# A twelve-stage decoder on one core: the position attention on row groups, and the history branch with channels on partitions

## The chip, the cores and the metric

One core of one Trainium2 chip runs the whole program. Its engines work side by side and are tied by semaphores: TensorE (PE, with its weight loads as PEld), VectorE (DVE), ScalarE (ACT), GpSimd (POOL) and SyncE (SP), which issues the DMAs. The metric is the device time of one execution in microseconds; the median of three runs is given. Of a profiled execution there is a trace, with the span from its first to its last instruction.

## The reference

Four decoder layers with three sublayers each (self attention, cross attention, feed forward), each followed by a layer norm of x plus its result. x is 8 batches of 100 tokens with 256 channels, the context 8 batches of 361 rows. Two sublayers matter here.

The feed forward of layer 1 begins with an attention of 16 heads of 16 channels that has relative positions:

```
x = _layernorm(src, ln1_g, ln1_b)
q, k, v = x @ wq, x @ wk, x @ wv         (16 heads)
p = (pe @ wp).reshape(2 * Ss - 1, H, HD)
ac = jnp.einsum('bihd,bjhd->bhij', q, k)
bd_full = jnp.einsum('bihd,phd->bhip', q, p)
rel = jnp.arange(Ss)[:, None] - jnp.arange(Ss)[None, :] + (Ss - 1)
bd = bd_full[:, :, jnp.arange(Ss)[:, None], rel]
att = jax.nn.softmax((ac + bd) * scale, axis=-1)
src = src + (att @ v) @ wo
x2 = _layernorm(src, ln2_g, ln2_b)       (then the experts)
```

There are 199 positions for 100 tokens, so bd_full is 100 x 199 for each head and batch, and each row of it is read shifted by one against the row above.

The cross attention of layer 2 takes from the context (the history) a summary for each batch, from which a small net makes 3x3 kernels for the attention scores:

```
eh = _gelu(_ln(historical_data @ hist_W + hist_b, hist_ln_g, hist_ln_b))   (361 x 512)
aw = _gelu(eh @ ctx_W1 + ctx_b1) @ ctx_W2 + ctx_b2                          (361)
aw = jax.nn.softmax(aw, axis=1)
cc = jnp.sum(eh * aw, axis=1)                                               (512)
```

## The kernel before

The stages (the functions in `STAGES`) run one after another. Each stage is one or more blocks; inside a block every engine has its own list of instructions, in the order written out by hand, and at the end of a block the engines meet. `stage_sems` gives a block its semaphores; with `looped=True` a block is repeated by a register loop (`Fori`), with a barrier of all engines between the turns. PSUM has 8 banks of 512 floats. Matmuls are in float32, and each stands in the trace as two records. The weights of the next stage are loaded by SP at the start of each stage.

**Position stage (`l1_ffn`, L2846).** In a first block the norm runs batch by batch (L2880 on), `pT` (positions times weights) is made, each batch is turned to channels on partitions (`x1T`), and then all queries are projected into `q1` (L2900, L2912). A loop of two turns with four batches each follows. In it GpSimd spreads the queries (L2937): for each head a copy of all 128 rows in which the other heads' rows are zero. TensorE multiplies each of the 16 heads with `pT` over all 128 rows (L2955), two heads in a PSUM bank; VectorE (L2927) and ScalarE (L2929) copy the banks in turn; SP stores each half batch to DRAM (L2972), in rows of 199 floats at a pitch of 200, and at the end of the turn waits until the stores have landed. The buffer `bd` holds two batches. After the loop `attention` (L184) runs, the generic one for all eight batches: it projects again, spreads the queries once more on GpSimd (L375), makes scores over 128 rows (L484), and adds the positions that SP loads back for each batch (L343), 100 floats at a time through the skewed view `skewed`; a separate instruction takes the maxima (L675, L678).

**The row-group attention (`self_heads`, L1172)** is used by the stages `l0_attn` and `l2_xattn`. It keeps the queries of even and odd heads apart in `q_pad`, so that a product needs only 32 rows; the four groups of 32 rows work on four banks (L1315). The masked scores and their maxima come from one instruction for each head (L1499), the exponentials from ScalarE (L1424), and turned probabilities are copied by VectorE and ScalarE in turn (L1508, L1433). What is small shares one side bank (projection of values L1279, inverses L1289, output L1294, turned x L1299), in the order of `side_order`.

**History branch (`l2_xattn`, L3201).** A first block loads the bias, gain and shift rows (`hist_rows`, on all partitions) and stores zeros for the taps. Then come two turns of a loop with four batches each. Tokens are on partitions, in three tiles of 121, 121 and 119. GpSimd copies the context (L3261), TensorE projects it (L3277), VectorE adds the bias, takes the statistics and normalises (L3341 to L3352), ScalarE applies gelu (L3320), TensorE turns the tiles to channels on partitions (L3287) and ScalarE copies them (L3324). The first layer (L3293), its gelu (L3327) and the logits (L3297, one row of 361) follow. The softmax runs on one partition (L3355 to L3362), its result is turned to a column (L3301, L3366), and TensorE sums the tokens of the four batches (L3306), 48 records with 512 columns over both turns. The result is turned to `ccT` (L3311, L3334). The block behind the loop makes the kernels from it (L3397 on).

## Time and profile before

| | us |
|---|---|
| median of 3 runs | 2757.68 |
| lowest, highest | 2756.59, 2758.4 |
| profiled execution | 2755.74 |
| its span | 2753.6 |
| PE busy | 2334.3 (85%) |
| PEld busy | 1864.6 (68%) |
| DVE busy | 1540.1 (56%) |
| ACT busy | 1138.2 (41%) |
| POOL busy | 516.5 (19%) |

The mean TensorE clock that was granted is 0.915 of full speed. Busy time is the union of an engine's instructions; TensorE's ends are modelled, so that a busy TensorE is not one at its peak. The shares are means over twelve stages with different limits, and a stage has to be read by itself.

### The profile page before, as it was taken

The numbers are of one execution on the slowest core, as the hardware profiler recorded it, in microseconds if no ns is written. First come the engines' busy times: TensorE is split into PE (matmuls) and PEld (weight loads), VectorE is DVE, ScalarE is ACT, GpSimd is POOL, SyncE is SP. The second block draws the span as 40 slices with busy tenths as digits, with TensorE's granted clock in tenths as the row PEclk, the third lists the DMA queues.
The fourth block names the chain that finished last, engine by engine and source line by source line (L and its number), as shares of the span: only waits on it lengthen the run. The fifth ranks groups of instructions, "written<-read, shape, count | busy, mean of one in ns | idle before, by whom it ended". The sixth has DMA issues, their size and how long they took to land. (4 is left out here: it accounts for less than half of the span.)

```text
span 2753.6 us, 43435 instructions
## 1 busy us (share of the span) xinstructions
PE 2334.3 (85%) x15392; PEld 1864.6 (68%) x15392; DVE 1540.1 (56%) x3310; ACT 1138.2 (41%) x3111; POOL 516.5 (19%) x715
## 2 busy tenths in 40 slices
PE   5799556669999966979787787979997999799997
PEld 3566322247777755879775336869995566599997
DVE  4566649984444432755556453545654556555555
ACT  5566345534334422623211233434332466455553
POOL 0200119961000023300133111000003222100000
PEclk9899779999999978979888888979997999799999
DMA  2000122210000034234200004422210000233332
GB/s 105 9 2 2 37 83 72 71 51 5 1 1 1 1 96 110 48 106 150 97 1 16 0 1 111 120 73 94 98 41 32 5 8 4 64 109 109 109 104 64
DMA packets 57520, 152.12 MB, mean 55 GB/s; under 512 B 16983, under 2 KB 31931, under 8 KB 55304
## 3 DMA queue, kind: packets, MB, share of 16 engines
q1 hardware_dynamic: 57356, 149.99, 17.4%
q8 instruction: 96, 1.57, 0.2%
q14 instruction: 68, 0.56, 0.1%
HBM read 138.48 MB, written 11.50 MB: 54 GB/s over the span
## 5 line engine op out<-in xcount | busy, mean ns | idle before, releaser
L2302 PE MATMUL ps<-l1a_zc,tables_sb 128*128 128x400 f32 x256 | 107.6, 553 | 96.3 <-POOL l1a_zc L2231 60.3
L2302 PEld LDWEIGHTS ps<-l1a_zc,tables_sb 128*128 128x128 f32 x256 | 46.9, 200 | 157.0 <-POOL l1a_zc L2231 88.5
L1799 ACT ACTIVATE l1x_probs<-ps,l1x_nmax 100x361 f32<-100x361 f32 x128 | 70.8, 558 | 189.1 <-DVE l1x_nmax L1881 189.1
L2242 POOL TENSOR_TENSOR l1a_dbx<-l1a_dx,l1a_rows 128x400 f32<-128x400 f32 x128 | 129.9, 1045 | 7.0 <-DMA l1a_rows<-l1a_rows_spilled 4.9
L2650 DVE TENSOR_TENSOR l3f_act_out<-l3f_act_out,l3f_gates 128x800 f32<-128x800 f32 x80 | 79.4, 992 | 81.9 <-ACT l3f_act_out L2606 81.9
L2654 DVE TENSOR_TENSOR l3f_hg_low<-l3f_act_out,l3f_hg_high 128x800 fp32r<-128x800 f32 x80 | 79.4, 993 | 62.9 <-ACT l3f_hg_high L2612 62.9
L2606 ACT ACTIVATE l3f_act_out<-ps,l3f_biases 128x800 f32<-128x800 f32 x80 | 74.4, 930 | 91.8 <-PE ps L2495 91.8
L2494 PE MATMUL ps<-l3f_x_high,l3f_w_high 128*128 128x400 f32 x320 | 111.4, 348 | 0.0
L2493 PE MATMUL ps<-l3f_x_high,l3f_w_low 128*128 128x400 f32 x320 | 110.7, 346 | 0.5 <-DVE l3f_w_low L2584 0.5
L2495 PE MATMUL ps<-l3f_x_low,l3f_w_high 128*128 128x400 f32 x320 | 110.8, 346 | 0.0
L2494 PE MATMUL ps<-l3f_hg_high,l3f_w_high 128*128 128x400 f32 x320 | 110.2, 344 | 0.0
L2255 ACT ACTIVATE ps<-l1a_delta,weights 128x400 f32<-128x400 f32 x128 | 76.5, 598 | 81.1 <-DVE ps L2285 53.1
L2493 PE MATMUL ps<-l3f_hg_high,l3f_w_low 128*128 128x400 f32 x320 | 110.1, 344 | 0.0
L2495 PE MATMUL ps<-l3f_hg_low,l3f_w_high 128*128 128x400 f32 x320 | 110.0, 344 | 0.0
L1024 ACT ACTIVATE l3x_probs<-l3x_s_sb,l3x_nmax 100x361 f32<-100x361 f32 x128 | 75.2, 589 | 70.3 <-DVE l3x_nmax L1113 66.3
L2612 ACT ACTIVATE l3f_hg_high<-l3f_act_out 128x800 fp32r<-128x800 f32 x80 | 70.0, 875 | 72.3 <-PE ps L2495 70.0
L1022 ACT ACTIVATE l0x_probs<-ps,l0x_nmax 100x361 f32<-100x361 f32 x128 | 70.8, 558 | 64.9 <-DVE l0x_nmax L1120 56.7
L2494 PE MATMUL ps<-l2f_x_high,l2f_w_high 128*128 128x400 f32 x272 | 95.0, 349 | 0.0
L2495 PE MATMUL ps<-l2f_x_low,l2f_w_high 128*128 128x400 f32 x272 | 94.4, 347 | 0.0
L2493 PE MATMUL ps<-l2f_x_high,l2f_w_low 128*128 128x400 f32 x272 | 94.3, 347 | 0.0
L2285 DVE TENSOR_TENSOR_SCAN ps<-ps,l1a_dbx 128x400 f32<-128x400 f32 x86 | 84.6, 994 | 16.6 <-POOL l1a_dbx L2242 9.8
L1113 DVE CUSTOM_DVE_ANT_0 l3x_s_sb<-ps,l3x_mask_b 100x361 f32<-100x361 f32 x128 | 63.2, 532 | 46.6 <-PE ps L929 46.3
(666 smaller groups left out, 6641.5 us busy)
## 6 DMA issues: line engine op xcount, KB each, us to landing
l3f_landing<-l_ffn_units SPq DMA_DIRECT2D x40, 513.0 KB, 3.4
l3f_gates<-l3f_gates SPq DMA_DIRECT2D x40, 400.0 KB, 3.5
l2x_a_taps<-l2x_taps_spread SPq DMA_DIRECT2D x8, 1912.5 KB
l2f_landing<-l_ffn_units SPq DMA_DIRECT2D x17, 771.0 KB, 4.3
l1a_rows<-l1a_rows_spilled SPq DMA_DIRECT2D x32, 400.0 KB, 3.2
l1f_gates<-l1f_gates SPq DMA_DIRECT2D x16, 800.0 KB, 4.2
l1f_positions<-l1f_bd SPq DMA_DIRECT2D x16, 621.9 KB
l1f_landing<-l_ffn_units SPq DMA_DIRECT2D x16, 512.0 KB, 3.5
```

The source lines that it names most:

```text
L1022: last = act.activation(probs[:, n % 2, r, 0:KEYS], score_bank(r), ACT.Exp, bias=nmax[:, n % 2, r:r + 1], accum_out=sums)
L1024: last = act.activation(probs[:, n % 2, r, 0:KEYS], s_sb[:, h % 3, r % 2, :], ACT.Exp, scale=-1.0, bias=nmax[:, n % 2, r:r + 1], accum_out ...
L2242: pool.tensor_tensor(dbx[:, n % BUFS, :], dx[:, j, m, :], rows[:, g % RING, 0, :], ALU.mult).then_inc(s.dbx_ready, 1)
L2255: act.activation(da(n), delta_h[:, m, j, :], ACT.Exp, scale=a_log[:, m, i:i + 1]).then_inc(s.da_ready, 1)
L2285: dve.tensor_tensor_scan(z(n), da(n), dbx[:, n % BUFS, :], 0.0, ALU.mult, ALU.add).then_inc(s.scan_done, 1)
L2302: pe.matmul(y_bank(m), st.ident, zc[:, n % DONE, :], start=(i == 0), stop=(i == NS - 1)).then_inc(s.sum_done, 1)
L2493: pe.matmul(out, r(w_lo), r(x_hi), start=start, stop=False)
L2494: pe.matmul(out, r(w_hi), r(x_hi), start=False, stop=False)
L2495: return pe.matmul(out, r(w_hi), r(x_lo), start=False, stop=stop)
L2606: act.activation(halves(act_out, t), st.ps[:, bank:bank + 2, 0:HALF], ACT.Gelu, bias=col(sl, 2 + t if geglu else t)).then_inc(s.gelu_done, 1)
L2650: dve.tensor_tensor(hg[:, t, :], act_out[:, t, :], gates[sl][:, 0, :], ALU.mult).then_inc(s.hg_gated, 1)
L2654: dve.tensor_tensor(hg_low[:, t, :].bitcast(F32R), hg[:, t, :], hg_high[:, t, :], ALU.subtract).then_inc(s.hg_ready, 1)
```

## The change

**Position stage.** The separate query projection, the loop over two turns and the call of `attention` are gone; `l1_ffn` calls `self_heads` with three new arguments: `xT` (the normed x, turned), `inner` (gain and shift of the second norm, and where its turned result goes) and `between` (the positions). The stage's norm block stays. In `self_heads` the products with the positions are made in 32 parts, four for each batch, each with four products over 32 rows (two row groups, two banks). The 12 parts of the first three batches stand ahead of the value projection and use four pairs of banks; those of batch j + 3 are woven into batch j, all in banks 0 and 1, which the scores use too, and each of them waits until both halves of the part before it are copied. VectorE copies the first bank of a part and ScalarE the second into `staged`, which holds three units of two parts. SP stores a unit in rows of 8 x 199 floats without a gap, and loads a batch of the skewed view into `bd` (two batches) when both its units have landed and the maxima of the batch two before are done. The position takes the place of the mask in the instruction of L1499. GpSimd adds the resid to x; VectorE's norm gets its gain and shift.

**History branch.** The first block and the loop become one block that runs all eight batches. Channels are on partitions: four products of 361 columns for each batch, straight from `ctxT`. The mean is taken out of the weights and of the bias beforehand (`w_centred`, `b_centred`), so that only the variance is left to find: VectorE squares, GpSimd adds the four channel tiles, TensorE sums over partitions into three columns, GpSimd raises to the power -0.5 and widens, TensorE spreads the result over all partitions. VectorE multiplies, and ScalarE's gelu takes gain and shift as its scale and bias. Logits are made on all 128 partitions. The exponentials of all batches and the weighted sums (VectorE, 32 with an accumulator) stand behind the loop. `hist_rows` is no longer loaded; three groups of four columns in the weights take its place.

The core of the diff (indentation halved):

```diff
-def self_heads(nc, st, name, w, bias=None, mask=None, conv=None):
+def self_heads(nc, st, name, w, bias=None, mask=None, conv=None, xT=None, inner=None, between=None):
...
+      bd_bank = lambda part: 2 * (part % 4) if part < 4 * AHEAD else 0
+      bd_tile = lambda part, i: st.ps[0:S, bd_bank(part) + i, 0:2 * REL]
+      staged_tile = lambda part, i: staged[:, part // 2 % STAGED, 4 * (part % 2) + 2 * i:4 * (part % 2) + 2 * i + 2, :].rearrange("q h r -> q (h r)")
...
+      def load(sp, j):
+        for unit in (2 * j, 2 * j + 1):
+          sp.wait_ge(bd_stored[unit % STAGED], 16 * (unit // STAGED + 1))
+        if j >= 2:
+          sp.wait_ge(s.masked_ready, G * (j - 1))
+        sp.dma_start(bd[:, j % 2], between.skewed(j)).then_inc(bd_loaded[j % 2], 16)
+      if between:
+        @block.sync
+        def _(sp):
+          for j in range(B):
+            if j >= AHEAD:
+              load(sp, j - 1)
+            for unit in (2 * j, 2 * j + 1):
+              sp.wait_ge(s.bd_first_copied, 2 * unit + 2)
+              sp.wait_ge(s.bd_second_copied, 2 * unit + 2)
+              sp.dma_start(between.rows(j)[:, (unit % 2) * (H // 2):(unit % 2 + 1) * (H // 2), :], staged[:, unit % STAGED]).then_inc(bd_stored[unit % STAGED], 16)
+            if j < 2:
+              load(sp, j)
+          for j in range(LOADED, B):
+            load(sp, j)
...
+        def positions(part):
+          j, q = divmod(part, 4)
+          m = q // 2
+          if part % (4 * HALF) == 0:
+            pe.wait_ge(s.q_even_copied, KT * (j // HALF + 1))
+            pe.wait_ge(s.q_odd_copied, KT * (j // HALF + 1))
+          if part >= 4 * AHEAD:
+            pe.wait_ge(s.masked_ready, G * (j - AHEAD) + 2)
+            pe.wait_ge(s.bd_first_copied, part)
+            pe.wait_ge(s.bd_second_copied, part)
+          elif part >= 4:
+            pe.wait_ge(s.bd_first_copied, part - 3)
+            pe.wait_ge(s.bd_second_copied, part - 3)
+          for par in range(2):
+            for i in range(2):
+              r = 2 * (q % 2) + i
+              group = slice(SLOT * r, SLOT * (r + 1))
+              last = pe.matmul(st.ps[0:S, bd_bank(part) + i, par * REL:(par + 1) * REL], q_pad[group, par, m, j, :], between.pT[group, m, :],
+                      start=True, stop=True, tile_position=(SLOT * r, 0))
+          last.then_inc(s.bd_ready, 1)
...
+          for part in range(4 * AHEAD):
+            positions(part)
+          pe.wait_ge(s.bd_first_copied, 4 * AHEAD)
+          pe.wait_ge(s.bd_second_copied, 4 * AHEAD)
         project("v", 0, 0)
...
             values(j - 1)
+          more = between and j + AHEAD < B
+          if more:
+            positions(4 * (j + AHEAD))
+          if 1 <= j <= B:
             on_the_side("inv", j - 1)
+          if more:
+            positions(4 * (j + AHEAD) + 1)
           if j < B:
             if conv:
               convolve(G * j + 2)
             turn(G * j)
+          if more:
+            positions(4 * (j + AHEAD) + 2)
           if j + 1 < B:
             on_the_side("v", j + 1)
           if j < KT:
             on_the_side("k", 1, j)
+          if more:
+            positions(4 * (j + AHEAD) + 3)
           if not conv and j + 1 < B:
             scores(j + 1)
...
+        def copy_positions(part):
+          act.wait_ge(s.bd_ready, part + 1)
+          wait_staged(act, part)
+          act.activation(staged_tile(part, 1), bd_tile(part, 1), ACT.Copy).then_inc(s.bd_second_copied, 1)
...
+          if between and r == 0:
+            dve.wait_ge(bd_loaded[j % 2], 16 * (j // 2 + 1))
           for n in range(G):
-            last = dve.tensor_tensor_reduce(s_sb[:, g % 3, n, :], score_bank(r)[:, n, :], conv.mask if conv else mask, 1.0, -3 * MASKED,
+            if between:
+              add = bd[:, j % 2, head(r, n), :]
+            else:
+              add = conv.mask if conv else mask
+            last = dve.tensor_tensor_reduce(s_sb[:, g % 3, n, :], score_bank(r)[:, n, :], add, 1.0, -3 * MASKED,
                             ALU.add, ALU.min, nmax[:, g % 3, n:n + 1])
...
-
-      w = weights(st, "f5")
-      attention(nc, st, "l1f", H, 16, False, w, xT=x1T, inner=InnerNorm(st.w["f5g2"][0:S, :], st.w["f5s2"][0:S, :], x2T), bd=skewed, per_turn=B)
-
+        return bass.AP(tensor=scratch.tensor, offset=b * S * PITCH + S - 1, ap=[[PITCH - 1, S], [REL, H], [1, S]])
+      self_heads(nc, st, "l1f", weights(st, "f5"), xT=x2T, inner=InnerNorm(st.w["f5g2"][0:S, :], st.w["f5s2"][0:S, :], x2T),
+           between=Between(pT=pT, rows=position_rows, skewed=skewed))
...
+          def widen(n):
+            pool.wait_ge(s.var_copied, n + 1)
+            pool.tensor_tensor(hrstd[:, n % 2, :], hvar[:, n % 2, :], st.minus_half[0:KROWS, 0:1].to_broadcast([KROWS, NT]), ALU.pow).then_inc(s.rstd_done, 1)
+            pool.wait_ge(s.rstd_done, n + 1)
+            if n >= 2:
+              pool.wait_ge(s.rstd_spread, n - 1)
+            pool.tensor_copy(rstd_wide[:, n % 2], hrstd[:, n % 2, :].unsqueeze(2).to_broadcast([KROWS, NT, P])).then_inc(s.rstd_widened, 1)
...
+          for n in range(B + 1):
+            if n < B:
+              pool.wait_ge(s.squared, 2 * n + 1)
+              pool.tensor_tensor(sq[:, n % 2, 0, :], sq[:, n % 2, 0, :], sq[:, n % 2, 1, :], ALU.add).then_inc(s.half_summed, 1)
+            if n >= 1:
+              widen(n - 1)
+            if n < B:
+              pool.wait_ge(s.squared, 2 * n + 2)
+              pool.tensor_tensor(sq[:, n % 2, 2, :], sq[:, n % 2, 2, :], sq[:, n % 2, 3, :], ALU.add).then_inc(s.half_summed, 1)
+              pool.wait_ge(s.half_summed, 2 * n + 2)
+              if n >= 2:
+                pool.wait_ge(s.var_ready, n - 1)
+              pool.tensor_tensor(sq_sum[:, n % 2, :], sq[:, n % 2, 0, :], sq[:, n % 2, 2, :], ALU.add).then_inc(s.sq_summed, 1)
...
+          def project(n):
             for c in range(CT):
+              if n >= 1:
+                pe.wait_ge(s.eh_copied, CT * (n - 1) + c + 1)
+              for k in range(KT):
+                last = pe.matmul(st.ps[:, c, 0:KEYS], w_hist[:, k, c * P:(c + 1) * P], st.ctxT[:, n, k, :], start=(k == 0), stop=(k == KT - 1))
+              last.then_inc(s.eh_ready, 1)
...
+          for n in range(B + 3):
+            if n < B:
+              project(n)
+            if 1 <= n <= B:
+              variances(n - 1)
+            if n >= 3:
+              if n == 3:
+                pe.wait_ge(s.w2_widened, 1)
+              attention_logits(n - 3)
+            if 2 <= n <= B + 1:
+              first_layer(n - 2)
+            if 1 <= n <= B:
+              spread(n - 1)
         @block.scalar
...
+          def copy_out(n, c):
+            act.wait_ge(s.eh_ready, CT * n + c + 1)
...
+            act.activation(buf(n)[:, c, :], st.ps[:, c, 0:KEYS], ACT.Identity, bias=b_centred[:, c:c + 1]).then_inc(s.eh_copied, 1)
+          def gelu(n, c):
+            if c == 0:
+              act.wait_ge(s.normed, n + 1)
+            act.activation(buf(n)[:, c, :], buf(n)[:, c, :], ACT.Gelu, scale=hg[:, c:c + 1], bias=hs[:, c:c + 1]).then_inc(s.eh_done, 1)
...
+          for n in range(B + 3):
+            old = n - 2
+            if n < B:
+              copy_out(n, 0)
+            if 0 <= old < B:
+              gelu(old, 0)
+              gelu(old, 1)
+            if n < B:
+              copy_out(n, 1)
+              copy_out(n, 2)
+            if 0 <= old < B:
+              gelu(old, 2)
+              gelu(old, 3)
+            if n < B:
+              copy_out(n, 3)
+            if 0 <= old < B:
+              gelu_first(old)
+          for n in range(B):
+            exponentials(n)
...
+          def normalise(n):
+            dve.wait_ge(s.rstd_spread, n + 1)
+            dve.wait_ge(s.squared, 2 * n + 2)
+            dve.tensor_tensor(buf(n), buf(n), st.ps[:, RSTD_BANK, 0:KEYS].unsqueeze(1).to_broadcast([P, CT, KEYS]), ALU.mult).then_inc(s.normed, 1)
+          def summary(n):
+            dve.wait_ge(s.aw_exp, n + 1)
+            for c in range(CT):
+              dve.scalar_tensor_tensor(buf(n)[:, c, :], buf(n)[:, c, :], 1.0, aw[:, n, :], ALU.mult, ALU.mult, accum_out=ccT[:, c, n:n + 1]).then_inc(s.cc_summed, 1)
...
+          for n in range(B + 3):
+            if 2 <= n <= B + 1:
+              normalise(n - 2)
+            if n < B:
+              square(n, 0)
+            if 1 <= n <= B:
+              copy_variances(n - 1)
+            if n < B:
+              square(n, 1)
+            if 3 <= n <= B + 2:
+              logits(n - 3)
+          for n in range(B):
+            summary(n)
```

## Rows read from the trace of the kernel before

**Rows 1.** Timeline of the position stage: start, us, engine, line [idle before <-releaser].

```profile
986.91 0.34 ACT L2909 ACTIVATE l1f_x1T<-ps 128x200 f32<-128x200 f32 x1 [0.90 <-PE ps L146]
...
1016.60 1.05 DVE L2927 COPY l1f_bd<-ps 100x398 f32<-100x398 f32 x2 [2.94 <-DMA l1f_positions<-l1f_bd]
...
1017.23 5.64 PE L2955 MATMUL ps<-l1f_pT,l1f_q_between 128*100 128x199 f32 x32 [0.81 <-DVE l1f_bd L2927]
...
1193.36 0.34 ACT L567 ACTIVATE l1f_x2T<-ps 128x200 f32<-128x200 f32 x1 [6.74 <-PE ps L459]
```

**Rows 2.** Busy us (x instructions) of PE, PEld, DVE, ACT, POOL; PEclk, DMA share, GB/s.

```profile
50.00:86.00 36.00, 27.82 (x404) 20.83 (x396) 27.41 (x176) 29.95 (x150) 5.54 (x15) 0.95 0.01 3
...
1012.00:1015.00 3.00, 3.00 (x20) 2.95 (x19) 0.89 (x2) 1.00 (x2) 1.08 (x1) 1.00 0.68 192
...
1069.00:1088.00 19.00, 6.31 (x31) 5.79 (x32) 0.00 (x0) 1.23 (x4) 5.85 (x4) 0.64 0.41 97
...
1085.00:1087.00 2.00, 2.00 (x7) 1.45 (x7) 0.00 (x0) 0.25 (x1) 2.00 (x2) 0.50 0.77 144
...
1088.00:1177.00 89.00, 81.17 (x789) 76.97 (x789) 67.62 (x144) 57.61 (x290) 29.66 (x32) 0.99 0.25 52
...
1495.00:1572.00 77.00, 62.16 (x188) 29.43 (x188) 41.05 (x88) 21.93 (x44) 13.14 (x16) 0.85 0.00 0
```

**Rows 3.** Waits of DVE and ACT in the two stages: us in total, times, longest.

```profile
DVE l1f_s_sb L675 <- DMA l1f_bd_cur<-l1f_positions: 20.1, 1, 20.1
...
ACT l2x_cc L3332 <- PE ps L3306: 31.2, 2, 15.6
```

**Rows 4.** Timeline of the history branch.

```profile
1489.36 0.44 POOL L3240 MEMSET l2x_zeros<- 100x408 f32 x1 [1.09 <-POOLq L88]
...
1537.33 1.41 DVE L3352 SCALAR_TENSOR_TENSOR l2x_eh<-l2x_eh,l2x_hrstd,l2x_hist_rows 119x512 f32<-119x512 f32 x2 [0.59 <-POOL l2x_hrstd L3267]
...
1544.49 5.13 PE L3293 MATMUL ps<-l2x_ehT,weights 128*128 128x361 f32 x16
...
1553.10 3.53 PE L3301 MATMUL ps<-tables_sb,l2x_aw 1*121 1x1 f32 x24 [2.06 <-DVE l2x_aw L3362]
...
1649.76 1.28 ACT L3411 ACT_TABLE_LOAD   x1 [0.80 <-PEq L88]
```

**Rows 5.** Timeline of the L0 attention.

```profile
14.83 7.56 PE L1274 MATMUL ps<-XT,weights 128*128 128x400 f32 x16 [14.83 <-PEq L3670]
...
24.80 0.26 DVE L1499 CUSTOM_DVE_ANT_0 l0a_s_sb<-ps,tables_sb 100x100 f32<-100x100 f32 x1 [1.08 <-PE ps L1315]
...
59.51 0.66 PE L1289 MATMUL ps<-tables_sb,l0a_rinv_wide 100*128 100x100 f32 x4 [0.72 <-POOL l0a_rinv_wide L1264]
...
61.63 0.96 PE L1315 MATMUL ps<-l0a_kT,l0a_q_pad 32*100 32x100 f32 x32
...
67.78 0.66 PE L1289 MATMUL ps<-tables_sb,l0a_rinv_wide 100*128 100x100 f32 x4 [0.71 <-POOL l0a_rinv_wide L1264]
...
111.19 0.34 ACT L1415 ACTIVATE XT<-ps 128x200 f32<-128x200 f32 x1 [5.38 <-PE ps L1299]
```

**Rows 6.** Groups by line: busy us, mean ns | idle before <-releaser; window as in rows 1, 5.

```profile
L2927 DVE COPY l1f_bd<-ps 100x398 f32<-100x398 f32 x32 | 18.0, 572 | 64.0 <-PE ps L2955 49.9 <-DMA l1f_positions<-l1f_bd 14.1
...
L2929 ACT ACTIVATE l1f_bd<-ps 100x398 f32<-100x398 f32 x32 | 15.6, 501 | 56.5 <-PE ps L2955 44.9 <-DMA l1f_positions<-l1f_bd 11.6
...
L1424 ACT ACTIVATE l0a_probs<-l0a_s_sb,l0a_nmax 100x100 f32<-100x100 f32 x128 | 46.5, 368 | 3.2 <-DVE l0a_nmax L1499 3.2
```

**Rows 7.** Groups by line: L1 stage, history branch.

```profile
L1784 ACT ACTIVATE l1x_kT<-ps,weights 128x361 f32<-128x361 f32 x64 | 35.9, 561 | 5.8 <-PE ps L1687 5.8
...
L1901 DVE TENSOR_TENSOR l1x_x_low<-ctxT,l1x_x_high 128x722 fp32r<-128x722 f32 x8 | 7.3, 910 | 13.4 <-ACT l1x_x_high L1819 13.4
...
L3267 POOL TENSOR_TENSOR l2x_hrstd<-l2x_hvar,minus_half 121x2 f32<-121x2 f32 x12 | 12.8, 1066 | 1.0
...
L2242 POOL TENSOR_TENSOR l1a_dbx<-l1a_dx,l1a_rows 128x400 f32<-128x400 f32 x128 | 129.9, 1045 | 7.0 <-DMA l1a_rows<-l1a_rows_spilled 4.9
```

More of the change, by code:

```diff
@@ L36 @@
 InnerNorm = namedtuple("InnerNorm", "gain shift turned")
+Between = namedtuple("Between", "pT rows skewed")
 Convolution = namedtuple("Convolution", "windows keep mask")
@@ L1193, in self_heads @@
         r_sb, o_norm = sb("r_sb", [P, 2, KT * S]), sb("o_norm", [P, 2, KT * S])
+        if inner:
+            norm.xnew = norm.resid
+        staged = sb("staged", [S, STAGED, H // 2, REL]) if between else None
+        bd = sb("bd", [S, 2, H, S]) if between else None
         kept = sb("kept", [S, 3, G, S + 2]) if conv else None
@@ L1437, in _ @@
                 copy_q(0)
+                if between:
+                    for part in range(4 * AHEAD):
+                        copy_positions(part)
                 for j in range(B + 2):
@@ L1451, in _ @@
                         copy_out("inv", j - 1)
+                    more = between and j + AHEAD < B
+                    if more:
+                        copy_positions(4 * (j + AHEAD))
                     if j == 0:
@@ L1527, in _ @@
                 copy_q(0)
+                if between:
+                    for part in range(4 * AHEAD):
+                        copy_positions(part)
                 copy_values(0)
@@ L1546, in _ @@
                         add_output(j - 2)
+                    more = between and j + AHEAD < B
+                    if more:
+                        copy_positions(4 * (j + AHEAD))
                     if j < B:
                         maxima(G * j + (1 if conv else 2))
+                    if more:
+                        copy_positions(4 * (j + AHEAD) + 1)
+                    if j < B:
                         if conv:
@@ L1551, in _ @@
                     if j >= 2:
-                        normalise_vector(dve, norm, s, j - 2)
+                        if inner:
+                            dve.wait_ge(s.x_summed, j - 1)
+                        normalise_vector(dve, norm, s, j - 2, *((inner.gain, inner.shift) if inner else ()))
                     if j < B:
@@ L3208, in l2_xattn @@
     w_k2 = st.w["a7kw2"].rearrange("p (k n) -> p k n", k=KT)
-    rows = [min(KROWS, KEYS - t * KROWS) for t in range(NT)]
     LINE = (3 * H + 2) * TAP_PITCH
@@ L3363, in _, with square @@
-                    for j in js:
-                        dve.wait_ge(s.p_turned, j + 1)
-                        for t in range(NT):
-                            dve.tensor_copy(pcol[0:rows[t], j, t, j:j + 1], st.ps[0:rows[t], bank(j, 0), t:t + 1]).then_inc(s.p_col, 1)
+                    def square(n, half):
+                        both = slice(2 * half, 2 * half + 2)
+                        dve.wait_ge(s.eh_copied, CT * n + 2 * half + 2)
+                        if n >= 2 and half == 0:
+                            dve.wait_ge(s.sq_summed, n - 1)
+                        dve.tensor_tensor(sq[:, n % 2, both, :], buf(n)[:, both, :], buf(n)[:, both, :], ALU.mult).then_inc(s.squared, 1)
```

377 lines of the change are left out of this document (151 added, 226 removed).

## The prediction

> **What bounds the kernel now.** I read the busy time by stretch first, to find the two stages that the change touches; then the waits inside them; then the timeline; then the durations of single instructions. Stages run one behind the other with a block switch between them, so the time of the program is the sum of its stages, and what a stage loses or gains moves everything behind it. Two stages count.
>
> The position stage runs from 987.25 (the last turned copy of the first norm ends) to 1193.70 (the last turned copy of the second) [rows 1]: 206.4 us. No engine is full in it outside 1088 to 1177, where TensorE is busy 81 of 89 us in the generic attention; from 1069 to 1088 it works 6.3 of 19 us at a mean clock of 0.64 [rows 2], and VectorE's first add waits 20.1 us for the first load of the skewed positions [rows 3]. So the stage is a front of some 100 us (query projection, two turns of the position loop with its stores drained at each end, block switches, first load), and 8 batches behind it.
>
> The history branch is entered at 1489.36 and the block behind it begins at 1649.76 [rows 4]: 160.4 us, in two like turns of 77 us. In one, TensorE is busy 62 us, VectorE 41, ScalarE 22 [rows 2]: the engines take turns, and ScalarE waits 31.2 us in two pieces for the weighted sums of L3306 [rows 3], which run with four result rows each.
>
> **The position stage after the change.** It removes the separate query projection, the masks of GpSimd, both turns of the loop and the generic attention; it adds the L0 stage's row-group attention with position products woven in. That attention is in the trace: from its first projection (14.83) to its last copy (111.53) are 96.7 us, 10.0 of them ahead of the first maxima at 24.80, and one batch in the steady middle takes 67.78 − 59.51 = 8.3 us [rows 5]. I put it at 987.25 + 1.05 for the block switch = 988.3.
>
> Front. The 12 parts of three batches are computed ahead of the first scores. Copies of query halves end at about +9 (24.80 − 14.83 less the value projection). A part is 8 records; the same product at 128 rows runs at 5.64/32 = 0.18 us a record [rows 1], 1.4 us a part in a row; but two row groups alternate, and four of them do the 32 records of the scores in 0.96 us [rows 5]. I take 0.9 for a part; bounds 0.7 and 1.6. The two copies (0.57 on VectorE, 0.50 on ScalarE [rows 6]) are beside each other. So three units (two parts each) are staged by about +14; the fourth copy has to wait for a store. Before, stores moved 192 GB/s and the load 144 GB/s [rows 2], so 637 KB take 3.4 us and 640 KB 4.4 us of transfer, and the first two stores, begun after the copies at 1006, were waited for until 1016.60 [rows 1]: I take 4 to 5 us from issue to landing. SyncE issues in order: store 0 and 1, then load 0, which waits for both (+17.5), and only behind it store 2; its landing (+22 to +25) frees the buffer for unit 5, whose copies end at +24 to +27; then come the value projection and the scores. The first maxima come at about +28 where L0 has +10: 18 us added. Bounds: 14 (the stores, in pieces eight times as long as before, are twice as quick) and 28 (each transfer takes 7 us).
>
> Batches. Five batches carry the products of a batch three ahead. I walk one, from the end of its scores, by the program's order. ScalarE: a turned copy behind TensorE's transposes (ends 1.1), the turned x (1.45), four exponentials of 0.37 [rows 6] (2.95), a turned copy (3.7). TensorE: values 0.9 (4.6), part 0 (5.5), inverse 0.7 [rows 5] (6.2). ScalarE: inverse copy, part copy (7.15). Part 1 until 8.1; ScalarE is in four exponentials until 8.65, its copy until 9.2; part 2 until 10.1. VectorE: copy of part 1 until 8.7, norm with gain and shift 1.4, four maxima of 0.26 [rows 5] 1.0, turned copy 0.6, so that its copy of part 2 ends at 12.2; part 3 until 13.1; copies until 13.7; the next scores 1.0. Sum 14.7 us. The path goes eight times between TensorE and the copiers, since all later parts share bank pair 0. Below it lie VectorE's own work (L0's 27.4 us in 36 [rows 2] are 6.3 a batch; 6.3 + 4 × 0.57 + 0.9 = 9.5 us) and the transfers (2 × 3.4 + 4.4 = 11.2 us); above it a serial part (4 × 0.5 more, 17). Five batches: 5 × (14.7 − 8.3) = 32. Three plain ones get 0.5 each for gain and shift, the last two norms 0.85 each: 3.2. End: 988.3 + 96.7 + 18 + 32 + 3 = 1138.2, against 1193.7: **55.5 us gained**; bounds 31 (front 28, batch 17, and the rest as it is) and 78 (front 14, batch 11).
>
> A rule that speaks against it: the Trainium skill, "TensorEngine Tiling (Array Packing)", Key Properties, says that a change of tiling mode drains the engine. Here the row-group scores start with no idle time ahead of them [rows 5]. Eight more changes in each of five batches, each costing one record of 0.18 us, would be 7 us.
>
> **The history branch after the change.** Removed: the first block's load and its switch (1489.36 to the loop), copies to hist_cur, transposes (c on the other axis now), one-row softmax and its turning, weighted sums on TensorE, the second turn's fill. TensorE per batch: 8 projection, 4 first-layer and 1 logit products of 361 columns, 26 records at 5.13/16 = 0.32 us = 8.3; three narrow variance products, 6 records at 3.53/24 = 0.15 = 0.9 [rows 4]; the spread, 6 records at 0.66/4 = 0.17 [rows 5] = 1.0. Together 10.2. ScalarE: 9 activations with bias at 0.56 [rows 7] = 5.0. VectorE: two squares at 0.91 [rows 7], one product of twice that width 1.8, variances and logits 1.3: 4.9. GpSimd: three adds of 361 columns (1.05 for 400 [rows 7]: 2.8), a power of three columns (1.07 for two [rows 7]: 1.6), widening 0.5: 4.9. All lie below TensorE's 10.2, and by the program's order each result is ready when TensorE asks (variances read squares of the batch before, first layer those of two before). So TensorE is the bound: 8 × 10.2 = 81.6.
>
> Around it: block start and the centring of weights on VectorE 4.0 (not in the trace; two to six); the first products at half clock, 3; the second iteration waits for the first power, 2.5; the drain (normalise, four gelus, first layer, gelu, logit, maximum) leaves bubbles of 4. Then a tail: all sums stand behind the last logits on VectorE, 32 of them. A like instruction of 512 columns takes 1.41/2 = 0.70 [rows 4], so 0.5 to 0.8 with its accumulator read; I take 0.6: 19.2. ScalarE's exponentials keep ahead of it. With 1.5 for the last steps and the switch: 4 + 3 + 2.5 + 81.6 + 4 + 19.2 + 1.5 = 115.8, against 160.4: **44.6 us gained**; bounds 30 and 55.
>
> **Sum.** The profiled execution took 2755.74 us (span 2753.6); 2755.7 − 55.5 − 44.6 = 2655.6. The median of the runs is 1.9 above it: 2657.6, so 2658.
>
> **Rivals.**
> **Quicker positions** (0.14): the copies find gaps, and a batch costs only the larger of VectorE and transfers, 11 (3.7 × 5 = 18.5 less), with a front 4 shorter. For it: before, one batch with products of all 128 rows took 11 us (89/8) [rows 2]. Against: the single bank pair. 55.5 + 18.5 + 4 = 78; time 2635.
> **Slower ring** (0.18): parts run serially and the SyncE order (a load that waits for maxima stands ahead of stores) holds the three-unit ring. 10 more in front, 14 in the batches: 2682. For it: before, the copies already waited for stores [rows 1].
> **Table switches** (0.04): if Identity with bias and Gelu did not share a table set, six loads of 1.28 us [rows 4] in each batch put ScalarE at 12.7 and, with the path, a batch at 13.5: 27 more, 2685. Against: no row shows the pair; the L1 stage has Identity with bias 64 times among exponentials at 0.56 us and 5.8 us of idle time in all [rows 7], so a second set is not needed there. The Trainium skill, "ScalarE: Activation LUTs", counts identity among the cheap functions that every set holds; by that rule the loop needs no load between them, which this trace cannot show.
> **Slower than before** (0.02): the granted clock stays at the lower level (1.2 GHz) in both stages. History: 10.2 more per batch, 82. Positions: some 6 us of the batch's path are TensorE's, 5 × 6 + 12 + 4 = 46. Together 128, net 28 slower: 2786. It decides from about three quarters of both stretches at that level. Against: 0.95 in L0's middle at 28 of 36 us busy, 0.85 in the history turn now [rows 2], which gets fuller.
>
> **How the numbers follow.** Forecast 0.60, with its own range 2640 to 2675; the rest is two in a hundred for terms of both stages falling together outside. The range runs from just below the quicker rival, 2632, to past the slower ones, 2692. This kernel's measurement tells 0.2% (5.5 us) from no change. Faster 0.97, same 0.01, slower 0.02.
>
> **What would show it.** Position stage near 150 us from its first norm copy: first maxima 28 after the first projection, maxima of batches one to four some 14.7 apart, the last three some 9; VectorE and ScalarE part copies waiting for TensorE, and in the front for stores. History: TensorE over 95% busy in the middle at clock 1.00, batches 10.2 apart, then 20 us of VectorE alone. Wrong if sums overlap the loop, if products of two row groups take over 1.4 us a part, if a table load stands between Identity and Gelu, or if the loop's pace is set by GpSimd.

## The result and the profile after

The changed kernel takes 2671.45 us (median of four runs, 2660.57 to 2675.93) against 2758.04 us for the kernel before on the same chip: a ratio of 0.968, 95% interval 0.965 to 0.971. Forecast were 2658, range 2632 to 2692. The profiled execution took 2672.13 us, its span is 2670.3 against 2753.6, so 83.3 us went. By stage:

| | before | after | gained | forecast |
|---|---|---|---|---|
| position stage, from the last turned copy of the first norm to that of the second | 206.4 | 173.3 | 33.2 | 55.5 |
| history branch, block start to next block | 160.4 | 105.4 | 55.0 | 44.6 |
| all stages ahead | 987.2 | 992.8 | −5.5 | 0 |
| between and behind | 1399.5 | 1398.8 | 0.7 | 0 |

The 5.5 us ahead are put down to scatter: the same instructions stand there, the stage's first projection begins anywhere from 987.3 to 995.3 us in the twelve profiles of this study that hold the new stage, and the run with the old stage and the new history branch reaches the end of the first norm at 992.4 too, where the kernel before had 987.2.

The head of the page of the changed kernel, busy time and two rows in 40 slices:

```profile
span 2670.3 us, 42999 instructions
...
PE 2268.9 (85%) x15178; PEld 1804.2 (68%) x15178; DVE 1497.1 (56%) x3444; ACT 1137.8 (43%) x3097; POOL 474.6 (18%) x697
...
PE   6799674659999976869987959899987999799998
...
PEclk8899787899999986669978979989988999799999
```

The sixteenth to eighteenth slices are the position stage: three 6s in the clock, where the page of before has no 6 at all. The same by stretch (columns as in [rows 2]): front; batches 0 and 1, which also carry the projections of batches 4 to 7; batches 2 to 4, the three others with parts (the recorded expectations call them "three to five"); and the rest.

```profile
992.80:1026.60 33.80, 17.78 (x144) 11.99 (x148) 7.72 (x15) 7.34 (x16) 0.95 (x1) 0.70 0.34 103
1026.60:1067.00 40.40, 32.67 (x204) 19.08 (x203) 14.40 (x81) 18.37 (x79) 0.40 (x1) 0.65 0.42 121
1067.00:1117.80 50.80, 41.44 (x399) 29.36 (x394) 27.51 (x141) 26.95 (x119) 5.45 (x12) 0.72 0.36 103
1117.80:1166.00 48.20, 34.18 (x324) 24.77 (x316) 27.09 (x143) 24.06 (x114) 8.76 (x19) 0.64 0.13 40
```

The third number from the end is the granted clock: 0.64 to 0.72, 0.68 over the whole stage, where L0's attention, from which I took the durations, has 0.95 [rows 2], and where the generic attention that was replaced had 0.99 [rows 2]. A clock of 0.68 is a mixture of TensorE's two levels, 2.4 and 1.2 GHz. The timeline of TensorE in one batch shows where it changes (start, us, engine, line, in brackets the idle time ahead and what ended it):

```profile
1104.82 0.89 PE L1423 MATMUL ps<-l1f_probsT,l1f_vals 100*32 100x100 f32 x32 [0.64 <-issue]
1105.65 0.92 PE L1367 MATMUL ps<-l1f_pT,l1f_q_pad 32*100 32x199 f32 x8
1107.38 0.66 PE L1337 MATMUL ps<-tables_sb,l1f_rinv_wide 100*128 100x100 f32 x4 [0.82 <-POOL l1f_rinv_wide L1308]
...
1110.79 1.65 PE L1367 MATMUL ps<-l1f_pT,l1f_q_pad 32*100 32x199 f32 x8
1112.38 2.03 PE L1327 MATMUL ps<-weights,l1f_xT 128*100 128x256 f32 x4
1114.34 1.65 PE L1367 MATMUL ps<-l1f_pT,l1f_q_pad 32*100 32x199 f32 x8
1116.66 1.67 PE L1387 MATMUL ps<-l1f_kT,l1f_q_pad 32*100 32x100 f32 x32 [0.68 <-DVE l1f_staged L1580]
```

L1367 is a part of the positions, L1327 the value projection, L1387 the scores. A part takes 0.92 us early in the batch (I had taken 0.9) and 1.65 us late in it, which is over the 1.4 us that I had named as a sign of being wrong; the scores take 1.67 instead of the 0.96 of [rows 5]. All these stand on the path, and the waits between them are short: none of TensorE's is over 0.92 us in these three batches. The last of the three took 17.3 us from scores to scores (1099.4 to 1116.7), the two ahead of it 15.6 and 17.2.

In the front, VectorE's copies of parts show the transfers (columns as in the timeline above):

```profile
1002.86 2.97 DVE L1580 COPY l1f_staged<-ps 100x398 f32<-100x398 f32 x6 [2.35 <-PE ps L1367]
1010.40 1.05 DVE L1580 COPY l1f_staged<-ps 100x398 f32<-100x398 f32 x2 [4.58 <-DMA l1f_positions<-l1f_staged]
1012.90 1.05 DVE L1580 COPY l1f_staged<-ps 100x398 f32<-100x398 f32 x2 [1.44 <-DMA l1f_positions<-l1f_staged]
1021.57 1.05 DVE L1580 COPY l1f_staged<-ps 100x398 f32<-100x398 f32 x2 [7.62 <-DMA l1f_positions<-l1f_staged]
...
1027.10 0.26 DVE L1615 CUSTOM_DVE_ANT_0 l1f_s_sb<-ps,l1f_bd 100x100 f32<-100x100 f32 x1 [1.93 <-PE ps L1387]
```

The first projection starts at 993.13, so the first maxima come 34.0 us behind it; L0 had 10, the forecast was 28.

The history branch, TensorE's timeline at its start and in the steady middle (L3328 projection, L3336 variances, L3343 logits, L3350 first layer, L3358 spread):

```profile
1465.54 12.88 PE L3328 MATMUL ps<-ctxT,weights 128*128 128x361 f32 x32 [1.59 <-DVE weights L3461]
...
1520.59 5.03 PE L3328 MATMUL ps<-ctxT,weights 128*128 128x361 f32 x16
1525.46 0.69 PE L3336 MATMUL ps<-l2x_ones,l2x_sq_sum 128*121 128x1 f32 x6
1526.02 0.85 PE L3343 MATMUL ps<-l2x_g1T,l2x_w_wide 128*128 128x361 f32 x2
1526.71 2.60 PE L3350 MATMUL ps<-l2x_eh,weights 128*128 128x361 f32 x8
1529.14 0.83 PE L3358 MATMUL ps<-tables_sb,l2x_rstd_wide 121*128 121x121 f32 x6
1529.80 5.03 PE L3328 MATMUL ps<-ctxT,weights 128*128 128x361 f32 x16
```

No gap, and 9.2 us from batch to batch. The first stretch below lies in this steady middle, the second behind the loop: there TensorE stands still, VectorE is full with the sums, and ScalarE has only 4 us of exponentials (columns as in [rows 2]):

```profile
1507.00:1520.00 13.00, 13.00 (x56) 8.84 (x55) 6.78 (x10) 6.09 (x12) 7.09 (x10) 1.00 0.01 2
...
1553.00:1568.30 15.30, 0.00 (x0) 0.00 (x0) 14.90 (x67) 3.98 (x15) 0.00 (x0) 0.51 0.00 0
```

VectorE's sums as a group (columns as in [rows 6]):

```profile
L3453 DVE SCALAR_TENSOR_TENSOR l2x_eh<-l2x_eh,l2x_aw 128x361 f32<-128x361 f32 x32 | 14.6, 529 | 0.0
```

### The profile page after: what moved, and what is told of

Its sections match the earlier page's. It is cut to its first block and busy times, and to the rows that moved or that the text cites. A ratio compares the mean times of both kernels' runs of the same rounds, so it can differ in the third digit from the quotient of the medians.

```text
span 2670.3 us, 42999 instructions
## 1 busy us (share of the span) xinstructions
PE 2268.9 (85%) x15178; PEld 1804.2 (68%) x15178; DVE 1497.1 (56%) x3444; ACT 1137.8 (43%) x3097; POOL 474.6 (18%) x697
## 3 DMA queue, kind: packets, MB, share of 16 engines
q1 hardware_dynamic: 46012, 149.21, 17.3%
```

## The experiments

Theory A: the position stage is 22 us longer than forecast because TensorE runs much of it at the lower clock, with a smaller part from the order of transfers in the front. Rival B: the path of copies through one bank pair and the transfers set the batch, and the clock is low because TensorE waits for them. Each ratio is to the kernel before on the same chip, with its 95% interval; "stage" is the time from the stage's first projection to the end of its last turned copy, 172.9 us in the changed kernel, and "block" the history branch's, 105.4.

| | median us | ratio | stage | block |
|---|---|---|---|---|
| changed kernel | 2671.45 | 0.9678 (0.9648 to 0.9709) | 172.9 | 105.4 |
| history branch alone | 2702.49 | 0.9793 (0.9778 to 0.9808) | | 105.1 |
| position stage alone | 2725.76 | 0.9882 (0.9864 to 0.9900) | | |
| products that nobody reads | 2657.63 | 0.9631 (0.9614 to 0.9647) | 164.5 | |
| their waits alone | 2670.68 | 0.9678 (0.9662 to 0.9695) | 178.1 | |
| store first | 2663.51 | 0.9652 (0.9639 to 0.9665) | 166.4 | |
| keys in front | 2660.58 | 0.9646 (0.9627 to 0.9665) | 167.4 | |
| keys and queries in front, store first, GpSimd's order | 2651.02 | 0.9613 (0.9595 to 0.9630) | 152.7 | 104.8 |
| sums in the drain | 2674.57 | 0.9682 (0.9659 to 0.9704) | | 107.4 |
| sums in the steady state | 2667.36 | 0.9679 (0.9657 to 0.9701) | | 105.7 |
| all together | 2641.96 | 0.9577 (0.9552 to 0.9601) | 146.7 | 107.3 |
| all, mended | 2639.90 | 0.9564 (0.9540 to 0.9589) | 142.7 | 105.3 |
| all, four units | 2641.73 | 0.9578 (0.9562 to 0.9594) | 144.3 | 105.6 |

**Each part of the change alone.** The one kernel keeps `l1_ffn` of before, the other `l2_xattn`.

> The history branch of the changed kernel with the position stage of the kernel before. Both theories of this study concern the position stage, so this run prices the two parts. If the traces' stage lengths are the two gains (history branch 105.4 us against 160.4 us, position stage some 33 us shorter), this kernel is 55 us below the kernel before, at 2703, and some 32 us above the changed kernel. If a part of the gain belongs to the clock that a stage leaves behind for the next, the difference is under 50 us.

> The position stage of the changed kernel with the history branch of the kernel before. If the two gains add, the history branch being worth 56.8 us by its own run, this kernel is at 2671 + 57 = 2728, some 30 us below the kernel before. If one stage leaves the other a better or worse clock, they differ from this sum by more than 4 us.

The history branch alone gives 56.8 us, the position stage alone 33.5; together 90.3, where the whole change gave 86.6 against the kernel before on its own chip. They agree with the stage lengths (55.0 and 33.2) and add within 4 us.

**Products that nobody reads, and the waits without them.** On TensorE, at five places of each batch:

```diff
+                def keep_busy(bank):
+                    if between:
+                        pe.matmul(st.ps[:, bank, 0:256], w.o[:, 0, 0:P], w.v[:, 0, 0:256], start=True, stop=True)
...
                 def values(j):
+                    if j > 0:
+                        pe.wait_ge(s.o_ready, j)
+                        keep_busy(O_BANK)
                     pe.wait_ge(s.even_copied, 2 * j + 2)
...
+                    if between and j + 1 < B:
+                        pe.wait_ge(s.masked_ready, G * (j + 1))
+                        keep_busy(3)
                     if more:
                         positions(4 * (j + AHEAD) + 3)
```

Each product goes to a bank that no other engine reads by then, and for that some waits move ahead of it. The second kernel has these waits with an empty `keep_busy`.

> Products whose results nobody reads, each 128 rows by 256 columns (some 0.55 us at the higher clock), are put in the position stage at the five places of a batch where TensorE waits: ahead of the values, of the inverse, of the second and the fourth part of the positions and of the scores. Theory A (the granted clock made my batch of 14.7 us one of 17.2): the clock of the stage rises from 0.70 to over 0.9, batches with parts take 14.5 to 15.5 us, the stage is 8 to 15 us shorter and the time is about 2661. Rival B (the path of copies and transfers sets the batch, the clock is low because TensorE waits): the five products lie partly on the path, the batch stays at 17 to 19 us and the time is 2671 to 2685.

> The waits of the run with products that nobody reads, moved as there (the values wait for the output first, and the fourth part and the scores for all maxima), without the products. If the products did it by way of the clock (theory A), this kernel is as the changed one: batches of 17.2 us, clock 0.70, scores at 1.67 us, time 2669 to 2673. If the other order of waits did it (rival B), batches three to five are at 14 to 16 us here too and the time is about 2661.

The stretches of batches 2 to 4 of both kernels, with the products and with the waits alone (columns as in [rows 2]):

```profile
1069.00:1113.20 44.20, 39.41 (x407) 26.80 (x406) 27.68 (x143) 27.30 (x119) 5.44 (x12) 0.95 0.38 114
```

```profile
1068.00:1124.00 56.00, 48.20 (x371) 33.55 (x367) 27.84 (x141) 27.28 (x119) 5.47 (x12) 0.57 0.31 90
```

With the products the clock is 0.95, the scores take 0.96 us, and the three batches take 14.0, 14.3 and 15.9 us; VectorE, ScalarE and GpSimd do the same work in both. With the waits alone the clock is 0.57 and the batches take 18.6, 17.2 and 20.3 us, 6 us more together than in the changed kernel, though the time is the same; of the 13.6 us of stage between the two kernels, 8.4 are therefore what the products gain over the changed kernel. The intervals of the two ratios don't meet: 13 us of time between kernels that differ only in work whose result is thrown away. That is theory A, and it shows my 14.7 us for a batch as right at the higher clock. What the products do not do is help batches 0 and 1: they stay at 21.3 and 20.6 us, at clocks of 0.61 and 0.67. There the projections of batches 4 to 7 (L1322) stand between copies, 5.3 us for the queries and 3.0 for each part of the keys, where L0 took 2.95 for the queries, 3.04 and 1.61 for the two parts of the keys.

**Store first.** SyncE issues the stores of units 2 and 4 ahead of the loads:

```diff
                             sp.dma_start(between.rows(j)[:, (unit % 2) * (H // 2):(unit % 2 + 1) * (H // 2), :], staged[:, unit % STAGED]).then_inc(bd_stored[unit % STAGED], 16)
-                        if j < 2:
-                            load(sp, j)
+                            if unit in (2, 4):
+                                load(sp, unit // 2 - 1)
```

> SyncE issues the store of unit 2 ahead of the load of batch 0, and that of unit 4 ahead of the load of batch 1. Theory C (SyncE's order holds the three-unit ring in the front): the store of unit 2 goes out at 7.5 us after the first store's place instead of 9.3, unit 5 is copied some 4 to 5 us earlier, the first maxima come 5 us earlier (29 us behind the first projection instead of 34) and the time is 2666.5. Rival D (the bytes set the front: three stores and one load have to pass whatever their order): the first maxima stay within 1 us of 34 and the time is 2670 to 2672.

VectorE's copies in that kernel, whose first projection starts at 988.27:

```profile
1005.54 1.05 DVE L1580 COPY l1f_staged<-ps 100x398 f32<-100x398 f32 x2 [4.68 <-DMA l1f_positions<-l1f_staged]
1008.25 1.05 DVE L1580 COPY l1f_staged<-ps 100x398 f32<-100x398 f32 x2 [1.67 <-DMA l1f_positions<-l1f_staged]
1010.86 1.05 DVE L1580 COPY l1f_staged<-ps 100x398 f32<-100x398 f32 x2 [1.56 <-DMA l1f_positions<-l1f_staged]
...
1016.39 0.26 DVE L1615 CUSTOM_DVE_ANT_0 l1f_s_sb<-ps,l1f_bd 100x100 f32<-100x100 f32 x1 [1.94 <-PE ps L1387]
```

The last pair of copies waits 1.56 us instead of 7.62, and the first maxima come at 28.1 instead of 34.0: theory C, 5.9 us. The batches behind are as before (21.1, 20.3, 17.1, 17.3, 17.3).

**Keys in front**, projected where TensorE waits for stores, instead of in batches 0 and 1:

```diff
+                    for part in range(KT):
+                        project("k", 1, part)
                     pe.wait_ge(s.bd_first_copied, 4 * AHEAD)
```

> The two projections of the keys of batches 4 to 7 move from batches 0 and 1 to the front, where TensorE waits for the third store's buffer. If they are why batches 0 and 1 take 20.2 us where 3 and 4 take 17.2, and the front hides them, batches 0 and 1 take some 17.2 us each and the time is 2665.5. If batches 0 and 1 are long because of the low clock and of transfers left over from the front, they stay at 19 to 20 us and the time is 2669 to 2673.

Batches 0 and 1 take 17.3 and 18.4 us instead of 21.1 and 20.1, for 0.8 us more in the front; the stage is 5.5 us shorter. The first outcome, though batch 1 keeps 1.2 us more. The time fell by 10.9 us, 5 more than forecast; the five single runs lie 14 us apart (2655.5 to 2669.5), so the stage in the profile says more here than the median.

**Front as a whole.** Store first; the second keys between parts 7 and 8, the second queries behind part 11; GpSimd widens inverse j + 1 ahead of the power of norm j (TensorE waited 0.82 us for it above).

> SyncE's order as in the run with the store first, both projections of batches 4 to 7 (keys and queries) in the front where TensorE waits for stores, and GpSimd widens the inverse ahead of the norm's power. No products that nobody reads. Forecast from the rows: front 27 to 29 us to the first maxima, batches 0 and 1 at 17 us instead of 21 and 20, 0.7 us less in each batch for GpSimd's order: stage 18 us shorter than in the changed kernel, time 2654. Theory A adds that the clock stays near 0.70. If the batches are set by transfers (rival B: 1.9 MB a batch at the 150 GB/s that the front reached are 12.6 us, and more if SyncE waits), they do not come below 17 and the time is 2660.

First maxima at 29.1, batches 13.7, 16.6, 16.5, 17.0 and 17.0; the stage is 20.2 us shorter, 2 more than forecast. Batch 0 came far below 17, so transfers don't hold it there, and rival B falls for batch 0 too; 16.6 for batch 1 would not settle it, but the mended kernel below has 15.0. The clock is 0.70 still in batches 2 to 4, and 0.64 and 0.60 in batches 0 and 1.

**Sums inside the loop.** In one kernel four exponentials stand behind ScalarE's ninth turn and their 16 sums in the last turns of VectorE; in the other three stand behind the sixth turn, with 12 sums in the turns that follow:

```diff
+                        if n == 5:
+                            for m in range(3):
+                                exponentials(m)
-                    for n in range(B):
+                    for n in range(3, B):
                         exponentials(n)
```

> History branch: the exponentials of batches 0 to 3 go behind the ninth turn of ScalarE's loop, and their 16 weighted sums behind the logits of the last two turns of VectorE's. Theory E (the tail of 32 sums at 0.455 us stands on the path and VectorE has room in the drain): the tail falls from 14.6 to 7.3 us, two table loads of 1.3 us on ScalarE come in, time 5 to 7 us less, about 2665. Rival F (the drain turns are chains through ScalarE, so that the exponentials and two table loads lengthen them by as much): 2670 to 2672.

> History branch: three exponentials (batches 0 to 2) at the end of ScalarE's sixth turn, in the full steady state, their 12 weighted sums spread over VectorE's turns 7 to 9; five batches stay behind the loop. In the steady state ScalarE has 9.2 less 5.4 us free in a turn and VectorE 9.2 less 4.8. If room in the steady state hides them (theory E, mended: only the drain was the wrong place), the loop keeps its pace, the tail falls by 12 x 0.455 = 5.5 us and the time is 2666. If a stop of 4.4 us on ScalarE (two table loads and three exponentials) is passed on to TensorE through the copies (rival F), 2 to 4 us of it come back and the time is 2668 to 2671.

Neither gained. In the first the exponentials and two table loads stood ahead of the last gelus, and TensorE shows it:

```profile
1550.59 5.15 PE L3350 MATMUL ps<-l2x_eh,weights 128*128 128x361 f32 x8 [4.96 <-ACT l2x_eh L3392]
```

It waited 4.96 us (1.70 in the changed kernel) and then ran at the lower clock, 5.15 us for a layer of 2.67: the block became 1.9 us longer. In the second the tail did fall by 5.5 us (last maximum to reciprocal 15.0 to 9.5), but ScalarE's stop was passed on. Its timeline:

```profile
1515.42 1.28 ACT L3402 ACT_TABLE_LOAD   x1
...
1519.02 1.28 ACT L3392 ACT_TABLE_LOAD   x1
1520.32 1.27 ACT L3392 ACTIVATE l2x_eh<-l2x_eh,weights 128x361 f32<-128x361 f32 x2
```

The turn of TensorE behind it took 10.9 us instead of 9.2, the drain waited for copies, squares and powers that were now late, and its first layer took 4.36 us at the lower clock; the last maximum came 5.7 us later than in the changed kernel. So the block is 0.3 us longer than in the changed kernel: rival F, and beyond its range, since not 2 to 4 us came back but all 5.5. The median of 2667.4 lies between the two forecasts, and its interval does not tell it from the changed kernel. The stop was 4.4 us; ScalarE is busy 4.9 us of the 9.2 in a turn (the expectation has 5.4, by adding durations that overlap), so that the room is 4.3, and that in more than one piece.

**All together.** All mended has the sums in the steady state and five more unread products in batch 0 (the expectation says six); the last kernel has four staged units.

> All together: store first, keys and queries in front, GpSimd's order, the five products a batch that nobody reads, and the sums woven in. If the gains add up and theory A holds also for batches 0 and 1, batches with parts take 14 us each (70 instead of 91), front 28, stage some 143 us instead of 172.6, sums 6 less: time 2636. If the products only move the clock where something else leaves room, 2645 to 2650.

> All together as before, with the sums in the steady state and six more products that nobody reads in batch 0, where TensorE waited and the clock fell to 0.60. If these keep the clock up, batches 0 and 1 fall from 14.9 and 18.3 us to 14 each and the time, with 7 us from the sums, is 2631. If batches 0 and 1 are short of clock for another reason, or the added products lie on the path, the stage stays at 146 us and the time is 2635 to 2638.

> The same with a ring of four staged units instead of three. If the ring holds copies back still (some copies of the front wait for stores: 4.7, 1.7 and 1.6 us on VectorE), the front is 3 to 4 us shorter and the time 2628. If the bytes set the front now, it is no shorter: 2631 to 2636, as the run with three units.

The position stage falls to 146.7 and 142.7 us. The mended kernel by stretch, front, batches 0 and 1, three to five, rest:

```profile
992.70:1021.90 29.20, 23.81 (x165) 14.46 (x165) 8.90 (x17) 9.42 (x20) 0.95 (x1) 0.86 0.38 118
1021.90:1047.00 25.10, 21.18 (x182) 14.13 (x182) 12.95 (x79) 16.43 (x75) 0.40 (x1) 0.93 0.56 162
1047.00:1091.00 44.00, 39.22 (x411) 27.17 (x410) 27.69 (x143) 27.30 (x119) 5.62 (x12) 0.95 0.44 134
1091.00:1135.40 44.40, 35.35 (x374) 26.10 (x374) 26.72 (x143) 24.39 (x114) 8.99 (x19) 0.88 0.17 48
```

The clock is 0.93 in batches 0 and 1, which take 11.2 and 15.0 us. The kernel without the five products had 14.9 and 18.2. Batch 0 and batch 1 from scores to scores, first without them, then with them:

```profile
1019.29:1034.23 14.94, 11.42 (x76) 7.20 (x76) 6.19 (x38) 7.77 (x36) 0.00 (x0) 0.63 0.59 166
1034.23:1052.47 18.24, 16.71 (x130) 11.71 (x129) 6.98 (x41) 8.88 (x39) 0.40 (x1) 0.65 0.40 117
```

```profile
1020.93:1032.08 11.15, 9.71 (x87) 6.44 (x87) 6.19 (x38) 7.66 (x36) 0.00 (x0) 1.00 0.58 176
1032.08:1047.08 15.00, 12.47 (x128) 8.56 (x129) 6.83 (x41) 8.77 (x39) 0.40 (x1) 0.89 0.56 159
```

The position stages differ in nothing else, and the other engines do the same work: theory A holds for batches 0 and 1 as well, with 7.0 us. The stage as a whole is only 4.0 us shorter, because the batches behind took 2.6 us more and the front 0.4 in this profile.

The times missed the forecasts of 2636, 2631 and 2628 by 6 to 14 us; 6 to 7 of each were sums that gave nothing. Four units brought the first scores forward (24.1 us behind the first projection instead of 28.2), but the first maxima came at 28.7 instead of 29.2: VectorE waited 4.85 us for the first load, the second outcome. That the bytes set the front now fits this and is not shown by itself. The early scores also cost something: TensorE then stood 4.2 us until the first maxima, its clock was 0.64 and 0.70 in batches 0 and 1, and from the first maxima to the end the stage took 115.6 us instead of 113.5. The three kernels can't be told apart by their intervals; each is faster than the changed kernel by about 1%.

## Why the prediction was right and where it was not

The time came 13 us above the forecast, inside the range. That it came so near is in part luck: errors of opposite sign met. In the profile (2672.1 against 2655.6): position stage 22.3 us too good, history branch 10.4 too bad, and 5 us from stages that were not changed.

**Position stage, batches: the step that failed.** "I walk one, from the end of its scores, by the program's order ... Sum 14.7 us." Order, waits and durations at the higher clock hold: 14.0 and 14.3 us with the clock at 1.00. The failure is to carry L0's durations, read at a clock of 0.95, into a stage with 0.68. From the first maxima to the end the stage took 138.9 us; the forecast's terms for that part (L0's 86.7, 32 and 3.2) are 121.9. So 17 us are missing. L0's scores show where:

```profile
23.77 0.96 PE L1315 MATMUL ps<-l0a_kT,l0a_q_pad 32*100 32x100 f32 x32 [0.52 <-DVE l0a_vals L1479]
...
45.24 0.96 PE L1315 MATMUL ps<-l0a_kT,l0a_q_pad 32*100 32x100 f32 x32
...
69.91 0.96 PE L1315 MATMUL ps<-l0a_kT,l0a_q_pad 32*100 32x100 f32 x32
```

With 6.4 us for the parts of each batch, the forecast has 34.3 us for batches 0 and 1, 43.9 for batches 2 to 4 and 44.8 for the rest. The changed kernel took 41.2, 50.1 and 49.4; with products that nobody reads the last two are 44.2 and 45.9, within 1.4 us of the forecast together. My fourth rival priced a position stage wholly at the lower level at 46 us more; at a mean of 0.68, 0.64 of the stretch is at that level, 29 us by the same price, against these 17. So the mechanism was seen, and I gave it 0.02 because I tied it to both stages and to the whole of them. It happened in one stage, in part. That the clock causes it is shown for batches 2 to 4 by the pair with and without products, 13.6 us of stage between them. For batches 0 and 1 place and clock both count: moving projections out gives 5 us for the keys and 11 with the queries and GpSimd's order, and with that order the clock is worth 7.0 us, by the two kernels that differ in five products. How the 7 us that the changed kernel lost there divide was not separated. The lower bound of 31 us for the stage's gain is a wrong sum besides: its terms, 10 us more in front and 5 × 2.3 in the batches, give 34. The measured 33.2 lies below what my terms allowed.

**Front.** "I take 4 to 5 us from issue to landing" was too short, because transfers share the queue (no row here shows one alone): the first store had landed 6.5 us behind its issue, both 8.9 us behind it, and store 2, issued just behind load 0, took 8.3 us, 1013.25 to 1021.57. So the first maxima came at 34.0, not 28. The order (store 2 behind load 0, unit 5 behind store 2) was right and is shown by the run with the store first. That DMA runs are longer now brought no clear gain in speed: from 1006 to 1011 us, with the first two stores under way, 197 GB/s moved, where [rows 2] had 192 for the short ones.

**Row groups.** A part took 0.92 us at the higher clock, 0.9 forecast (ten in a row in the front took 4.90 us, so that they overlap; at the lower clock one takes 1.65), and starts without idle time behind products of another shape (1105.65 above). By "TensorEngine Tiling (Array Packing)", Key Properties, of the Trainium skill, a change of mode drains the engine; no row here shows a stop for it, as [rows 5] showed none.

**History branch.** TensorE is the bound at clock 1.00 without a gap, as forecast. The batch is 9.2 us, not 10.2: I charged the narrow products by their busy time in [rows 4] and [rows 5], but followed by others they overlap (from variances to logits 0.56 us, not 0.9; the spread 0.66, not 1.0; logits and first layer 3.13, not 3.2; projection 4.87, not 5.1). That is 8 us of the 10.4. The tail was 14.6 us instead of 19.2: a sum takes 0.529 us and its accumulator read 0.082, but the next starts 0.455 behind. That is 4.6. Against them, the first products at the lower clock and the waits of the drain took 13.8 us where I had 9.5, and start and end took 2.1 us less than forecast. No table load stands between Identity and Gelu: in ScalarE's whole loop there is one, at its first gelu (1485.76 us, 1.28 us long). The Trainium skill, "ScalarE: Activation LUTs", section "Table sets: the hidden batching unit", says that cheap functions, identity among them, appear in every set; the trace agrees for the set of the gelu. GpSimd's 0.86 us for the power of three columns and 0.82 for an add stay below the bound: it is busy 3.9 of 9.2 us in a turn.

## What to carry to other kernels

A duration read in one stage holds for the clock of that stage: write the granted clock beside each duration of TensorE, and when a path of short products between copies replaces a full TensorE, price it at both levels, in part as well as in whole. Work moved into a pipeline's steady state is hidden only if the whole stop, table loads included, fits the room between two uses of that engine; the sums gained 5.5 us in the tail and lost as much ahead of it. And when transfers share a queue, take their bytes together, and see which store another engine waits for before a load is put ahead of it.

## What the hardware showed that was not expected

More work for TensorE made the kernel faster: against the same waits without them, five unread products in a batch took the clock of batches 2 to 4 from 0.57 to 0.95 and 13 us off the time; five in batch 0 alone took its clock from 0.63 to 1.00. The clock fell in batches in which no wait of TensorE's in the timeline was over 0.92 us, so it is not only long pauses that cost it. The same code reached the same instruction anywhere between 987.3 and 995.3 us in twelve profiles; what moves it was not looked for. And single runs of the mended kernel lie 22 us apart (2629.4 to 2651.0), those of the kernel before 12 us (2753.9 to 2766.3) in more runs. That a stage near the change of the clock makes the time less sharp would explain it; no run tested it, and the kernel with the new position stage alone, whose stage has the same mean clock of 0.68, speaks against it with four runs within 4.0 us.
